# First LayerNorm and Hadamard step: the shift row moved from VectorE into an accumulating matmul, the sign vector folded into the matrix

## The reference, cut to what matters

```python
def _layernorm(x, axis=-1, eps=1e-5):
    m = jnp.mean(x, axis=axis, keepdims=True)
    v = jnp.var(x, axis=axis, keepdims=True)
    return (x - m) / jnp.sqrt(v + eps)

# ffn
    x = fwht(x * SU_ug) / SCALE
    x_up = x @ W_up.T * (Wscale_ug[:INTER] * SCALE)
    x_gate = x @ W_gate.T * (Wscale_ug[INTER:] * SCALE)
    x = jax.nn.silu(x_gate) * x_up
    x = fwht(x * SU_dp) / SCALE
    x = x @ W_down.T * (Wscale_dp * SCALE)

# layer
    x = _layernorm(x + _L0_attn_ref(x, ...), axis=-1)
    x = _layernorm(x + _L0_ffn_ref(x, ...), axis=-1)
```

## Time and profile before

| | |
|---|---|
| two timed runs | 3171.66 and 3174.42 us, median 3173.04 |
| the profiled execution | 3169.24 us |
| its span, slowest core (core 2) | 3168.2 us; the eight cores 3153.5 to 3168.2 |
| mean granted TensorE clock | 0.923 to 0.924 on every core |
| busy: TensorE, VectorE, ScalarE | 2633.4 (83%), 594.1 (19%), 636.1 us (20%) |
| chain that ended last | TensorE 77%, DMA 9%, VectorE 6%, ScalarE 4% |
| the loop over 16 chunks | first L588 at 1379.73 us, last L604 from 1478.33 for 1.23 us |
| behind it to the second Hadamard matmuls | until 1519.67 us |

### The profile page before, as it was taken

One profiled execution on the slowest core, in us unless ns is written; L12 is line 12 of the kernel. 1 busy time (PEld: TensorE's weight loads), 2 busy tenths in 40 slices (PEclk: granted clock), 3 DMA queues, 4 the chain that ended last, 5 costly groups with the idle time before them and its releaser, 6 DMA issues.

```text
span 3168.2 us, 28802 instructions; the slowest of 8 cores (3153.5 to 3168.2 us)
## 1 busy us (share of the span) xinstructions
PE 2633.4 (83%) x11024; PEld 1038.3 (33%) x11024; DVE 594.1 (19%) x626; ACT 636.1 (20%) x616; POOL 114.6 (4%) x203
## 2 busy tenths in 40 slices
PE   3999994989999999721299999999999649999970
PEld 1444441222222222200044444444444214444430
DVE  0222220111111111154211111111111230000014
ACT  0000000665556655610000000000000130000010
POOL 1000000000000000000000000000000000000000
PEclk9999996999999999955599999999999879999985
DMA  9348646001010000003444444444444483554426
GB/s 152 72 77 138 110 90 197 3 1 40 1 40 1 1 1 1 1 23 60 153 96 88 99 88 95 94 90 97 87 97 89 117 186 80 120 114 100 106 59 206
DMA packets 120421, 258.76 MB, mean 82 GB/s; under 512 B 34784, under 2 KB 75744, under 8 KB 115168
## 3 DMA queue, kind: packets, MB, share of 16 engines
q0 software_dynamic: 54960, 149.54, 27.6%
q1 hardware_dynamic: 64376, 102.13, 10.1%
q10 hardware_dynamic: 952, 5.24, 0.7%
HBM read 337.19 MB, written 58.72 MB: 125 GB/s over the span
## 4 chain that ended last, share of the span: by engine, by line
PE 77%; DMA 9%; DVE 6%; ACT 4%; issue 2%; another core or an unknown queue 1%; POOL 0%; DVEq 0%; SPq 0%; ACTq 0%; POOLq 0%
PE ps_ug L164 29%; PE ps_y L164 14%; PE ps_ring L164 14%; PE ps_o L404 7%; PE ps_d L400 6%; PE ps_s L164 5%; DMA AR<-scr_f 2%; DMA ARF<-xkvA 1%; DMA ARF<-scr_f 1%; DMA out<-stg_f 1%; ACT AR L456 1%; DMA ARF<-xq 1%; ACT stg_b L456 1%; PE ps_f L164 1%
## 5 line engine op out<-in xcount | busy, mean ns | idle before, releaser
L164 PE MATMUL ps_ug<-AR,QSB 128*128 128x512 bf16 x2688 | 590.4, 379 | 0.0
L164 PEld LDWEIGHTS ps_ug<-AR,QSB 128*128 128x128 bf16 x2688 | 263.0, 98 | 317.2
L164 PE MATMUL ps_ug<-AR,WBUF 128*128 128x512 bf16 x1408 | 312.7, 381 | 13.3 <-DMA WBUF<-WgateT 13.3
L164 PE MATMUL ps_s<-QSB,AR 128*128 128x512 bf16 x768 | 236.0, 391 | 76.4 <-DMA AR<-scr_vt 44.0
L713 ACT ACTIVATE stg_b<-ps_ug,sgate 128x1024 bf16<-128x1024 f32 x64 | 71.3, 1114 | 826.0 <-PE ps_ug L164 826.0
L164 PE MATMUL ps_y<-ARF,QSB 128*128 128x512 bf16 x1024 | 225.0, 381 | 4.1 <-issue 4.1
L164 PE MATMUL ps_ring<-ARF,AR 128*128 128x512 bf16 x768 | 170.7, 384 | 53.4 <-DMA ARF<-xkvA 53.4
L400 PE MATMUL ps_d<-AR,ones_b 128*1 128x512 bf16 x512 | 196.6, 384 | 11.0 <-DVE rowbuf L418 11.0
L404 PE MATMUL ps_o<-AR 128*128 128x512 bf16 x512 | 202.5, 395 | 0.0
L456 ACT ACTIVATE AR<-ps_s,biasB_sb 128x1024 bf16<-128x1024 f32 x160 | 177.9, 1112 | 107.7 <-PE ps_o L404 107.7
L164 PEld LDWEIGHTS ps_ug<-AR,WBUF 128*128 128x128 bf16 x1408 | 138.1, 98 | 181.4 <-issue 16.6
(11 more groups left out here) (106 smaller groups left out, 1507.3 us busy)
## 6 DMA issues: line engine op xcount, KB each, us to landing
QSB<-WdownT POOLq DMA_DIRECT2D x16, 2048.0 KB, 16.4
QSB<-WupT POOLq DMA_DIRECT2D x42, 512.0 KB, 5.1
QSB<-WgateT POOLq DMA_DIRECT2D x42, 512.0 KB, 7.1
ARF<-xkvB POOLq DMA_DIRECT2D x8, 2048.0 KB, 18.8
scr_f<-QSB SPq DMA_DIRECT2D x64, 256.0 KB, 2.0
WBUF<-WupT POOLq DMA_DIRECT2D x22, 512.0 KB, 5.1
WBUF<-WgateT POOLq DMA_DIRECT2D x22, 512.0 KB, 7.1
ARF<-xkvA POOLq DMA_DIRECT2D x4, 2048.0 KB, 40.1
```

The costliest lines, as they stand in the source:

```text
L164: return pe_.matmul(out_ap, lhsT, rhs, start=start, stop=stop, skip_group_check=True)
```

## The change

- Ahead of the loop VectorE makes a bf16 copy `subf` of the 2048 signs (128 x 16), and in 16 instructions writes into `masks` sixteen matrices `h128` whose rows are multiplied by the signs of chunk c. Each waits for the one before.
- TensorE multiplies each column of `subf` with `h128` (16 matmuls, 128x1 weights, 128 columns), into row 0 of `ps_bc`; VectorE copies the 2048 results to `hsut` (one partition, bf16).
- Then `ps_a` is filled with two f32 matmuls; `ps_b` is no longer made. VectorE writes a bf16 copy `browb` of `brow`.
- In the loop VectorE multiplies the chunk by `ps_a` in place; the addition and the sign multiplication are gone. ScalarE copies the chunk to bf16. TensorE runs two matmuls for each half: the signed matrix on the chunk, and, added to it in PSUM, a matmul with one row of weights (`hsut`, 1x128) and one row of data (`browb`, 1x512).
- `ARF`, and so `scr_xh`, holds the chunk without its `brow` part; that part is one number for each token, which the second LayerNorm takes out again.

```diff
--- before.py
+++ after.py
@@ -550,14 +550,45 @@
                   nc.psum_tensor("ps_f", [128, 2048], F32) as ps_f_t):
                 ps_a, ps_b = ps_bc[:, 0:1024], ps_bc[:, 1024:2048]
                 ps_f = [ps_f_t[:, i * 1024:(i + 1) * 1024] for i in range(2)]
-                pe_bc = ln_bcast(ps_a, ps_b, d5)
+
+                subf = AR1[:, 18432:18448]
+                p.w(dv_, "dv")
+                dsub = p.inc(dv_.tensor_scalar(subf, suug[:, :], 1.0, None,
+                                               ALU.mult), "dv")
+                for c in range(KC):
+                    p.w(dv_, "dv")
+                    p.inc(dv_.tensor_scalar(masks[:, c * 128:(c + 1) * 128],
+                                            h128[:, :], suug[:, c:c + 1], None,
+                                            ALU.mult), "dv")
+                dv_hs = p.v("dv")
+                p.w(pe_, "dv", dv_hs)
+                for c in range(KC):
+                    inst = pe_.matmul(ps_bc[0:1, c * 128:(c + 1) * 128],
+                                      subf[:, c:c + 1], h128[:, :],
+                                      start=True, stop=True,
+                                      skip_group_check=True)
+                pe_hs = p.inc(inst, "pe")
+                hsut = AR1[0:1, 16384:18432]
+                p.w(dv_, "pe", pe_hs)
+                dv_hsut = p.inc(dv_.tensor_copy(hsut, ps_bc[0:1, 0:2048]), "dv")
+                p.w(pe_, "dv", d5)
+                p.w(pe_, "dv", dv_hsut)
+                for half in range(2):
+                    inst = pe_.matmul(ps_a[:, half * 512:(half + 1) * 512],
+                                      ones_fr[:, :],
+                                      arow[:, half * 512:(half + 1) * 512],
+                                      start=True, stop=True,
+                                      skip_group_check=True)
+                pe_bc = p.inc(inst, "pe")
+                browb = rowbuf[:, 0:512].bitcast(BF16)
+                p.w(dv_, "dv")
+                dv_bb = p.inc(dv_.tensor_copy(browb, brow), "dv")
 
                 tsl = [stg_b[:, 1024:2048], stg_b[:, 2048:3072]]
                 f1sl = [stg_b[:, 0:1024], stg_b[:, 3072:4096]]
                 tsl_done = [0, 0]
                 f1_done = [0, 0]
                 f1_evac = [0, 0]
-                tmp = stg_f[:, 1024:2048]
                 t2 = AR1[:, 0:KC * T]
                 f1r = scr_f1.rearrange("c (h j) t -> h c (j t)", h=8)
                 rd_q = [(0, 0, 0)] * 4
@@ -581,22 +612,26 @@
 
                 p.w(dv_, "pe", pe_bc)
                 p.w(ac_, "ac")
+                p.w(ac_, "dv", dv_bb)
                 for c in range(KC):
                     ch = ARF[:, c * T:(c + 1) * T]
                     sb = c % 2
                     p.w(dv_, "dv")
-                    p.inc(dv_.tensor_tensor(tmp, ch, ps_a, ALU.mult), "dv")
-                    p.w(dv_, "dv")
-                    p.inc(dv_.tensor_tensor(ch, tmp, ps_b, ALU.add), "dv")
-                    p.w(dv_, "dv")
-                    p.w(dv_, "pe", tsl_done[sb])
-                    dvt = p.inc(dv_.tensor_scalar(tsl[sb], ch, suug[:, c:c + 1],
-                                                  None, ALU.mult), "dv")
-                    p.w(pe_, "dv", dvt)
+                    dvt = p.inc(dv_.tensor_tensor(ch, ch, ps_a, ALU.mult), "dv")
+                    p.w(ac_, "dv", dvt)
+                    p.w(ac_, "pe", tsl_done[sb])
+                    acv = p.inc(ac_.copy(tsl[sb], ch), "ac")
+                    p.w(pe_, "ac", acv)
                     p.w(pe_, "dv", f1_evac[sb])
                     for half in range(2):
-                        inst = mm(ps_f[sb][:, half * 512:(half + 1) * 512], h128[:, :],
-                                  tsl[sb][:, half * 512:(half + 1) * 512], True, True)
+                        mm(ps_f[sb][:, half * 512:(half + 1) * 512],
+                           masks[:, c * 128:(c + 1) * 128],
+                           tsl[sb][:, half * 512:(half + 1) * 512], True, False)
+                        inst = pe_.matmul(
+                            ps_f[sb][:, half * 512:(half + 1) * 512],
+                            hsut[:, c * 128:(c + 1) * 128],
+                            browb[:, half * 512:(half + 1) * 512],
+                            start=False, stop=True, skip_group_check=True)
                     pev = p.inc(inst, "pe")
                     tsl_done[sb] = pev
                     p.w(dv_, "pe", pev)
```

## The result

| | before | changed |
|---|---|---|
| median of all runs, us | 3172.51 (35 runs) | 3179.15 (36 runs) |
| ratio to the kernel before | | 1.0017, 95% interval 1.0011 to 1.0024 |
| profiled execution, us | 3169.24 | 3178.56 |
| its span, slowest core | 3168.2, core 2 | 3177.5, core 0 |
| L527's start to the first loop instruction (every core) | 8.7 | 15.8 |

The change made the kernel slower by 0.17%, which is 5.4 us (3.5 to 7.6). The first LayerNorm and the loop grew by 8.5 us on each of the eight cores.

The account below looks back on a forecast made before the run. Bound: a serial chain through loop and read-back, TensorE and VectorE not limiting. Preparation +7.6 and loop -0.2 give +7.4 us: 3176.6 against the profiled execution, 3180.4 as timed median; own range 3173 to 3187, wider range 3166 to 3190.

Parts of the forecast that it names:

- The bound: Loop and work ahead: one serial chain, nothing beside it to hide changes, so each microsecond moves everything behind by as much.
- The preparation: Ahead of the loop: new work all on the path, 15.1 us against 7.5, so 7.6 us lost (5.8 to 9.7).
- the sixteen matrices: Ahead of the loop: VectorE's signed matrices, each waiting for the last, 0.35 us each, 5.6 us (4.5 to 6.7).
- the two broadcasts: Ahead of the loop: two f32 matmuls in place of four, 3.9 us where four ran 7.33.
- The short matmuls: Ahead of the loop: hop, sixteen TensorE matmuls of 128 columns and a tail, 2.85 us (2.2 to 3.9).
- The loop: Sixteen chunks: period 6.23 us against 6.24, about 0.2 us gained (6 gained to 3.6 lost).
- The changes of shape: In the loop: three switches between 128x128 and one-row weights per chunk, 0.12 us each, 0.36 a chunk (bounds nothing and 0.2 each).
- The hops: In the loop: VectorE's multiplication to ScalarE 1.31 us, ScalarE's copy to TensorE 1.18 us, each including its instruction.
- Hidden shape changes: Rival, loop: one-row weight loads go under the running matmul; period 5.87, net +1.7 us, 3174.7; chance 22%.
- The clock: Rival, loop: more matmuls raise TensorE to 2.4 GHz; period 5.32, net -7.1 us, 3165.9; chance 8%.
- The unpipelined pair: Rival, loop: accumulating matmuls into one PSUM bank show their tails; period 6.89, +18 us net, 3191; chance 7%.
- The read-back: Rival, behind the loop: another meeting of the cores' transfers could add up to 10 us, 3190; chance 7%.

Follow-up runs that it names:

- prep_only: Kernel before, with the new preparation put unused ahead of its four broadcast matmuls; ratio 1.0030 to the kernel before, +9.5 us.
- hoist: Changed kernel with VectorE's preparation ahead of the statistics, short matmuls and `hsut` copy during ScalarE's square root; ratio 0.9989 to the kernel before, -3.5 us.
- pipe_after: Changed kernel with VectorE's multiplication of chunk c+2 ahead of chunk c's copy out of PSUM; ratio 0.9828 to the kernel before, -54.6 us.
- lean_waits: Changed kernel without two loop waits, on ScalarE's copy and TensorE's first matmul, that other waits imply; period 6.19 us, single execution 3181.9 us.
- group: Changed kernel with each chunk's two 128-row matmuls before both one-row ones; period 6.11 us against 6.33, single execution 3170.9 us.
- same_shape: Changed kernel with one-row matmuls replaced by repeats of the 128x128 ones, output not the reference's; period 6.01 us, single execution 3173.6 us.
- hoist_group_lean: Changed kernel with preparation ahead of the statistics, matmuls grouped by weight shape, two implied waits removed; ratio 0.9967 to the kernel before, -10.5 us.

## Why the prediction was right, point by point

**The bound.** A single file with nothing beside it: right. `prep_only` and `hoist` show that a microsecond ahead of the loop is a microsecond of the total within their intervals, and `pipe_after` that the loop's time was the order's.

**The preparation: 7.6 us forecast, 7.1 measured** (from 7.5 to 14.6, from L527's end). By its terms: `subf` 0.28 and 0.28; the sixteen matrices 5.6 and 5.7, 0.355 each. That number was right and its derivation was not: I put L593's 1.40 in place of 1.32 down to its scalar operand, but the first two L593, which have the same operand and only one wait, follow after 1.33, so the 0.07 there is more likely the price of a second wait, like those of `lean_waits`. No run takes that wait away from VectorE; it is argued from the jump at the third chunk. The matrices take 0.255 each where the row of 0.28 took 0.18; they have a scalar for each partition, but also 128 bf16 columns and not 64 of f32, so what the 0.07 more is paid for isn't shown. The right number came by luck. `hsut` 2.44 and 2.43; the two broadcasts 3.9 and 3.9. The short matmuls were the one term off: 2.85 forecast, 2.1 measured. They start 0.107 us apart, and their weight loads don't show; the lower bound was the value.

**The loop: 0.2 us gained forecast, 1.4 lost measured.** The period came out at 6.33 for 6.23. The changes of shape were 0.107 us for 0.12, so the attention rows did carry over to the lower clock, neither vanishing nor doubling. The hops were too small: I took 1.31 and 1.18 from instructions with one wait, and these have two from the third chunk on, 1.37 and 1.29. That is 0.17 in a chunk, and `lean_waits` gives it back. The trace of before had it to be read: its first two chunks take 6.00 us and nearly all later ones 6.24, and the first copy out of PSUM follows 1.11 behind the matmuls where the earlier trace rows has 1.19. Kernel before, core 2, first chunk (its L588 is at 1379.73):

```profile
1383.29 1.01 PE L164 MATMUL ps_f<-stg_b,h 128*128 128x512 bf16 x2 [3.73 <-DVE stg_b L593]
1384.40 1.22 DVE L604 CAST stg_b<-ps_f 128x1024 bf16<-128x1024 f32 x1 [1.27 <-PE ps_f L164]
...
1385.73 1.22 DVE L588 TENSOR_TENSOR stg_f<-ARF,ps_bc 128x1024 f32<-128x1024 f32 x1
```

**The rivals.** Hidden shape changes: refuted by `group` and `same_shape`. The rule of the Trainium skill ("TensorE: Matmul & The Clock Gate", Part 2), that the next weight load is pulled ahead under a running matmul, agrees with these traces where the shapes are equal (the load at 1445.36 for the matmul at 1445.79 in `same_shape`, 0.43 between starts) and not across a change between 128-row and one-row weights (the load at 1481.80 for the matmul at 1481.81, 0.53). The clock: 0.50 as forecast, though not for the forecast's reason, which was that TensorE would be idle for two thirds of the time: in `pipe_after`, busy 9.79 of 10 us, it was 0.50 too. The unpipelined pair: refuted, no tail shows between the four. The read-back: its mean over the cores is 115.0 us for 114.6, with a spread from 108 to 124 in one execution.

**The total: +7.4 forecast, +5.4 (3.5 to 7.6) measured.** The stage grew by 8.5, a little more than the interval of the total holds. The forecast for the stage was 7.4: 0.5 too much for the preparation and 1.6 too little for the loop, errors of opposite sign, so a part of the total's good fit is luck. Whether the 3 us between them are chance or something given back between cores stays open. No experiment settles it: `prep_only` had 10.9 in the stage and 9.5 (5.7 to 13.6) in the total, `hoist_group_lean` -7.5 and -10.5 (-14.6 to -6.3).

## What to carry to other kernels

Before moving work off an engine, look whether that engine or the program's order sets the period: in a serial chain an instruction moved elsewhere is still in the chain, with a hop more. First let the next chunk's first step stand ahead of this chunk's last; then the same edit, which cost 5 us here, brings about 30. Constant preparation belongs where its engine is idle, and matmuls with differently shaped weights belong in groups.

## What the runs showed of the hardware that I had not expected

- A wait that is already met wasn't free where it was an instruction's second: 0.06 us on ScalarE, 0.11 on TensorE (6.36 us a chunk with them and 6.19 without).
- VectorE instructions of 1.22 us with no wait on each other start 1.13 us apart; with one, 1.32.
- One-row matmuls kept TensorE's granted clock at 0.50 through a loop in which it was busy 9.79 of 10 us; 128-row ones in their place let it rise to 0.76 in the same stretch.
- Changing between 128-row and one-row weights costs 0.107 us at 1.2 GHz. Attention's rows, at a granted clock of 1.00, have about 0.10 for a change, mostly between 128-column and one-column weights; so the cost was about the same at both clocks.
- A large write beside a read-back held up its last group (22 to 24 us behind the third, 8 without the write), and taking it away didn't bring the first group sooner.
